# The attention output product of a one-core RWKV and feed-forward kernel in three fp32r passes, moved behind the first value tile

## The reference

```python
x = x + 0.5 * ffn(layernorm(x))            # ffn: one 256x256 matrix, summed from 8 chosen adapters, and a bias
x = x + attn(layernorm(x))
x = x + 0.5 * ffn(layernorm(x))

def attn(x):                               # x: 8 x 512 x 256
    h = layernorm(x) * ln1_g + ln1_b
    hh = time_shift(h)                     # the token before, zero for the first
    k, v = mix(h, hh, tm_k) @ Wk.T, mix(h, hh, tm_v) @ Wv.T
    sr = sigmoid(mix(h, hh, tm_r) @ Wr.T)
    rwkv = sr * wkv(time_decay, time_first, k, v)   # a scan over the tokens
    x = x + rwkv @ Wo.T                    # the output product of this case; its sum is xa below
    h = layernorm(x) * ln2_g + ln2_b
    hh = time_shift(h)
    kk = square(relu(mix(h, hh, cm_k) @ Wck.T))     # 1024 wide
    return x + sigmoid(mix(h, hh, cm_r) @ Wcr.T) * (kk @ Wcv.T)
```

## Time and profile before

| | |
|---|---|
| median of 3 runs | 430.83 us (430.48 to 431.03) |
| the profiled execution | 430.12 us, span of its instructions 428.0 us |
| TensorE clock granted over the span | 0.997 of full speed |
| PE busy | 414.6 us, 97% |
| DVE busy | 372.2 us, 87% |
| ACT busy | 334.7 us, 78% |
| POOL busy | 181.9 us, 43% |

### The profile page before, as it was taken

The page is one execution under the profiler, slowest core; times in us unless marked ns, Lnnn a source line. Parts: engine busy times, 40 slices in busy tenths (PEclk is TensorE's granted clock), DMA queues, the critical chain, the costliest instruction groups (busy, mean ns, idle before and its releaser), DMA issues.

```text
span 428.0 us, 6400 instructions
## 1 busy us (share of the span) xinstructions
PE 414.6 (97%) x2074; PEld 335.9 (78%) x2074; DVE 372.2 (87%) x735; ACT 334.7 (78%) x679; POOL 181.9 (43%) x194
## 2 busy tenths in 40 slices
PE   8989989989999999999999999999999999999996
PEld 8865875668867887798769886788779876988895
DVE  3988989997989899998989898989999898979555
ACT  1158977899699969998799969996999479956830
POOL 1446062817173454617281727345461518043011
PEclk9999999999999999999999999999999999999998
DMA  6991010001000001000200020000000000000011
GB/s 202 394 397 67 2 49 0 2 1 52 0 0 2 25 18 58 0 26 1 76 0 2 25 74 2 0 25 20 7 2 25 2 25 0 2 25 27 0 51 50
DMA packets 15971, 18.52 MB, mean 43 GB/s; under 512 B 1082, under 2 KB 13634, under 8 KB 15938
## 3 DMA queue, kind: packets, MB, share of 16 engines
q1 hardware_dynamic: 14538, 17.05, 11.3%
q10 hardware_dynamic: 1400, 1.07, 0.9%
HBM read 13.92 MB, written 4.19 MB: 42 GB/s over the span
## 4 chain that ended last, share of the span: by engine, by line
PE 75%; DVE 2%; issue 1%; POOL 1%; ACT 0%; DVEq 0%; POOLq 0%
PE pair L490 21%; PE pair L368 10%; PE pair L380 10%; PE pair L464 6%; PE pair L465 6%; PE pair L468 6%; PE pair L358 6%; PE pair L349 4%; PE pair L434 1%; PE pair L435 1%; PE pair L438 1%; PE pair L511 1%; PE pair L510 1%; PE pair L514 1%; PE pair L528 0%
## 5 line engine op out<-in xcount | busy, mean ns | idle before, releaser
L490 PE MATMUL pair<-wcv_sb,kk 128*128 128x256 f32 x448 | 100.4, 380 | 0.0
L490 PEld LDWEIGHTS pair<-wcv_sb,kk 128*128 128x128 f32 x448 | 83.8, 190 | 11.4 <-ACT kk L755 0.7
L464 PE MATMUL pair<-xck_hi,wck_hi 128*128 128x512 f32 x128 | 54.8, 428 | 0.0
L468 PE MATMUL pair<-xck_lo,wck_hi 128*128 128x512 f32 x128 | 50.7, 396 | 0.0
L465 PE MATMUL pair<-xck_hi,wck_lo 128*128 128x512 f32 x128 | 50.6, 395 | 0.0
L751 ACT ACTIVATE kk<-pair 128x512 f32<-128x512 f32 x64 | 36.3, 589 | 14.6 <-PE pair L468 14.5
L1407 POOL TENSOR_TENSOR x2b<-xs,bias_bc 128x512 f32<-128x512 f32 (+1 forms) x16 | 20.0, 1253 | 56.0 <-DVE xcr L1117 33.2
L755 ACT ACTIVATE kk<-kk 128x512 f32<-128x512 f32 x64 | 36.3, 624 | 0.0
L1407 POOL TENSOR_TENSOR x<-x,bias_bc 128x512 f32<-128x512 f32 x14 | 18.1, 1298 | 40.8 <-DVE xcr_lo L1165 22.3
L1447 POOL TENSOR_TENSOR xs<-x,xa 128x512 f32<-128x512 f32 x16 | 20.4, 1273 | 33.7 <-DVE xa L1098 33.7
L1433 POOL TENSOR_TENSOR xr<-xr,h 128x512 f32<-128x512 f32 x16 | 19.2, 1222 | 28.4 <-ACT xr L811 28.4
(11 more groups left out here) (181 smaller groups left out, 1135.1 us busy)
## 6 DMA issues: line engine op xcount, KB each, us to landing
x<-in_x_dram SPq DMA_DIRECT2D x8, 512.0 KB, 4.2
out_dram<-xs SPq DMA_DIRECT2D x15, 256.0 KB, 2.1
xt<-in_xt_dram SPq DMA_DIRECT2D x4, 512.0 KB, 7.4
work<-in_ffn_w_dram ACTq DMA_DIRECT2D x4, 256.0 KB, 4.3
work<-in_ffn_w_dram SPq DMA_DIRECT2D x4, 256.0 KB, 4.6
kk<-in_wck_dram SPq DMA_DIRECT2D x1, 1024.0 KB, 10.6
xs<-in_xt_dram SPq DMA_DIRECT2D x2, 512.0 KB, 11.6
wcv_sb<-in_wcv_dram SPq DMA_DIRECT2D x1, 1024.0 KB, 13.3
```

Source lines behind the costliest of these rows:

```text
L464: nc.tensor.matmul(key_bank(n), wck_hi[:, h, cols], xck_hi[:, h, :], start=h == 0, stop=False)
L468: last = nc.tensor.matmul(key_bank(n), wck_hi[:, h, cols], xck_lo[:, h, :], start=False, stop=h == CH - 1)
L490: last = nc.tensor.matmul(bank_of("kv", e, i)[:, t % TB * C:(t % TB + 1) * C], kk[:, n, tok:tok + P], wcv_sb[:, n, :], start=n == 0, stop= ...
```

## The change

Weights: `wo_sb` (already scaled by 0.5) gets a high part `wo_hi` (ACT, `setup_wo_high`, in the place of three constants of the start, which are gathered in the tile `early`) and a low part `wo_lo` (DVE, `output_weight_rest`, in place). Item 0 keeps the fp32 product. For items 1 to 7 `rwkv` gets a high part on ACT (`output_input_high`, two instructions between square 6 and square 7 of kk) and a low part on POOL (`output_input_rest`, two instructions, behind the second bias sum of x), and the product is 24 fp32r matmuls: for each of the two token tiles of a bank, the matmuls with `rwkv_hi` for both banks first, then those with `rwkv_lo`. Both banks are signalled by the last matmuls of the whole.

PE: `output_product(f)` stands behind the whole tile 0, `turn_xa(f)` in the middle of tile 2. ACT: squares 4 to 6 come before the high part of rwkv, square 7 and the residual before the gate's tanh; one of the squares of x2 moves behind the high part of xv. POOL: the bias sum into the second half of x2b (of item e - 1) moves from behind the small inverses to directly behind the inverse root of xa. Semaphores are merged where one could serve twice; such lines are left out below.

```diff
-        centre_own = sb("centre_own", [P, P])
-        centre_other = sb("centre_other", [P, P])
+        early = sb("early", [P, 2 * P + C])
+        centre_own, centre_other, bias_sel = early[:, 0:P], early[:, P:2 * P], early[0:K, 2 * P:2 * P + C]
...
+        wo_hi, wo_lo = in_place_of("early", "wo_hi", [P, CH, C]), in_place_of("wo_sb", "wo_lo", [P, CH, C])
...
+        rwkv_hi, rwkv_lo = in_place_of("xr", "rwkv_hi", [P, CH, T]), in_place_of("rwkv", "rwkv_lo", [P, CH, T])
...
             def output_product(f):
                 if f == 0:
                     pe.wait_ge(s_wo, 1)
-                pe.wait_ge(rwkv_done, 2 * f + 2)
-                to_tokens("o", rwkv, wo_sb, xa2_done, f, o_ps)
+                    pe.wait_ge(rwkv_done, 2 * f + 2)
+                    to_tokens("o", rwkv, wo_sb, xa2_done, f, o_ps)
+                    return
+                if f == 1:
+                    pe.wait_ge(s_wo_lo, 1)
+                pe.wait_ge(rwkv_hi_done, 2 * (f - 1) + 2)
+
+                for t in range(TB):
+                    toks = [slice((i * TB + t) * P, (i * TB + t + 1) * P) for i in range(BANKS)]
+                    dsts = [bank_of("o", f, i)[:, t * C:(t + 1) * C] for i in range(BANKS)]
+                    for i in range(BANKS):
+                        if t == 0:
+                            take(pair_of("o", f), i, xa2_done, 2 * f + i + 1)
+                        for h in range(CH):
+                            nc.tensor.matmul(dsts[i], rwkv_hi[:, h, toks[i]], wo_hi[:, h, :], start=h == 0, stop=False)
+                            nc.tensor.matmul(dsts[i], rwkv_hi[:, h, toks[i]], wo_lo[:, h, :], start=False, stop=False)
+                    for h in range(CH):
+                        if t == 0:
+                            pe.wait_ge(rwkv_lo_done, 2 * (f - 1) + h + 1)
+                        for i in range(BANKS):
+                            last = nc.tensor.matmul(dsts[i], rwkv_lo[:, h, toks[i]], wo_hi[:, h, :], start=False, stop=h == CH - 1)
+                            if t == TB - 1 and h == CH - 1:
+                                last.then_inc(o_ps, 1)
...
                 if e == LAST:
                     break
-
-                channel_values(e, 0, range(HB // 2))
+                channel_values(e, 0)
                 if has(f):
                     output_product(f)
-                channel_values(e, 0, range(HB // 2, HB))
                 channel_values(e, 1)
+
+                channel_values(e, 2, range(HB // 2))
                 if has(f):
                     turn_xa(f)
-                channel_values(e, 2)
+                channel_values(e, 2, range(HB // 2, HB))
...
+            def setup_wo_high():
+
+                act.wait_ge(s_ffn_ps, 1)
+                act.wait_ge(s_wo, 1)
+                nc.scalar.activation(wo_hi[:, :, :], wo_sb[:, :, :], ACT.Copy).then_inc(s_wo, 1)
+
+            def output_input_high(f):
+                act.wait_ge(r_ps, 2 * f + 2)
+                for h in range(CH):
+                    act.wait_ge(rwkv_done, 2 * f + h + 1)
+                    nc.scalar.activation(rwkv_hi[:, h, :], rwkv[:, h, :], ACT.Copy).then_inc(rwkv_hi_done, 1)
...
+                if h == 0 and 0 <= f - 2 < SUMS_X2:
+
+                    act.wait_ge(var_done["x2"], NT * (f - 2) + TB)
...
             keep_first(5)
+            setup_wo_high()
             setup_wv()
...
+                if has(f):
+                    value_input_high(f)
+                    scaled_difference(f)
                 if 0 <= e - 1 < SUMS_X2:
                     squares_x2(e - 1, (1,))
-                if has(f):
-                    value_input_high(f)
-                    scaled_difference(f)
...
                 for n in range(1, HB // 2):
                     key_square(e, n)
+                for n in range(HB // 2, HB - 1):
+                    key_square(e, n)
+                if has(f):
+                    output_input_high(f)
+                key_square(e, HB - 1)
+                if has(f):
+                    residual_of(f)
                 channel_gate(e)
-                if has(f):
-                    residual_of(f)
-                for n in range(HB // 2, HB):
-                    key_square(e, n)
...
+            def output_weight_rest():
+                dve.wait_ge(s_wo, 2)
+                dve.wait_ge(o_ps, CH)
+                nc.vector.tensor_tensor(wo_lo[:, :, :], wo_sb[:, :, :], wo_hi[:, :, :].bitcast(F32), ALU.subtract).then_inc(s_wo_lo, 1)
...
             norm_output(0)
+            output_weight_rest()
             stats_x1(1)
...
+            def output_input_rest(f):
+                for h in range(CH):
+                    pool.wait_ge(rwkv_hi_done, 2 * (f - 1) + h + 1)
+                    nc.gpsimd.tensor_tensor(rwkv_lo[:, h, :], rwkv[:, h, :], rwkv_hi[:, h, :].bitcast(F32), ALU.subtract).then_inc(rwkv_lo_done, 1)
...
                     bias_to_x(f + 1, 1)
+                if has(f):
+                    output_input_rest(f)
+                if has(f + 1):
                     lower("x1", f + 1 - SUMS_X1, x1_done, 2 * (f + 1) + 2)
                 if has(f):
                     attention_sum(f, 0)
                     attention_sum(f, 1)
                     inverse_std("xa", f)
+                if has(e - 1) and e < LAST:
+
+                    bias_to_x2(e - 1, 1)
                 if has(f + 1):
                     first_inverses(f + 1)
                 if has(f + 2):
                     inverse_x(f + 2)
-                if has(e - 1) and e < LAST:
-                    bias_to_x2(e - 1, 1)
```

28 lines of the change are left out of this document (14 added, 14 removed).

## The result

| | us, median (range), runs |
|---|---|
| before | 430.83 (430.29 to 431.06), 5 |
| changed | 443.38 (443.01 to 445.39), 5 |
| ratio | 1.030, 95% interval 1.0285 to 1.0314 |
| predicted | 439.1, range 433.3 to 442 |

The change makes the kernel 12.6 us slower, 4.3 more than predicted and outside the range. The profiled execution of the changed kernel took 445.39 (span 443.5); its other four have spans of 441.1 to 441.7, so about 2 us of it is this one execution's. They stand in the start: TensorE waited 2.33 us for its first `normed` (before 1.23), and behind that the granted clock from 24 to 32 us was 0.79 (before 1.00), so part of this stretch ran at 1.2 GHz instead of 2.4.

A forecast was written before the change was run, and what follows sets the result against it. TensorE, busy 97% of the span, was taken as the bound. Product -4.4, chain to the turned xa +11.4, tile 0 wait +1.2 and start +0.1 gave +8.3 us: 439.1 us predicted, range 433.3 to 442.

The forecast's parts named there:

- The chain from the product to the turned xa: Output product to xa's transposes: banks finishing together and the moved bias add holding up normalisation make TensorE wait, +11.4 us.
- The first rival: At xa's normalisation: GpSimd's bias add does not hold it up, giving 433.5 us; chance 9%.
- The product: Output product in items 1 to 7: 24 fp32r matmuls take 2.82 us instead of 3.45, -4.4 us.
- The 2.62 us: Output product time by the skill's 109 ns per matmul; not used, it would make the sum 1.4 us lower.
- The wait inside tile 0: Value tile 0: TensorE waits for ScalarE's eighth square, 0.2 us an item in items 2 to 7, +1.2 us.
- "No wait" for the low part: Output product: GpSimd's low parts of rwkv are ready in time, with 0.3 us to spare.
- The third rival: GpSimd's low parts meet VectorE's adds of the next x1, 0.5 us in seven items: 442.6 us; chance 9%.
- The start: Before item 0: VectorE's weight subtraction stands ahead of the mix, +0.1 us.
- The forecast's own range: Total time with the wait in tile 0 between its bounds: 437.5 to 441 us.
- Behind the turning there is room: After xa's transposes: mixing and high/low parts need about 4.7 us, TensorE has 5.18 of values first; nothing charged.

The follow-up runs named there:

- e15: Changed kernel with ScalarE's old order of the x2 squares and the output product done bank by bank: 434.76 us.
- e1: Changed kernel with GpSimd's second-half bias add for x2 put back behind the two small inverses: 446.12 us.
- e5: Kernel before, with only GpSimd's second-half bias add for x2 moved directly behind the inverse for xa: 433.08 us.
- e9: Changed kernel with one wait added: GpSimd's mixing of xr waits until both low parts of xv are done on VectorE: 439.89 us.
- e2: Changed kernel with the second half of the x2 squares back ahead of xv's high copy and the scaled difference on ScalarE: 439.34 us.
- e4: Kernel before, with only the x2 squares' second half moved behind xv's high copy and the scaled difference, plus the wait this needs: 430.62 us.
- e10: e3 with GpSimd's mixing of xr waiting for both low parts of xv: 440.38 us.
- e3: Changed kernel with both GpSimd's bias add for x2 and ScalarE's x2 squares back in their old places: 444.25 us.
- e16: e2 with xa turned after six of the third value tile's eight summands instead of four: 444.59 us.
- e17: e16 with the second token tiles of the output product done bank by bank: 441.26 us.
- e18: e17 with GpSimd's mixing of xr waiting for both low parts of xv: 436.19 us.
- e23: Changed kernel, old squares order, product bank by bank, rwkv's low part on VectorE, mixing of xr waiting for xv's low parts, xa turned after five summands: 430.53 us.

## Why the prediction was right and wrong

**The chain from the product to the turned xa (+11.4): right**, 11.5 measured, each link within 0.05 us in items 3 to 7. Item 2 lost 2.14 us instead of 1.83: its first add of xa starts 0.42 us behind the semaphore that it waits for, and not 0.07 as everywhere else. That is so in all twelve kernels in which GpSimd makes the low part of rwkv and in none of the others; no row says why. That alternating banks cost the other part is shown by e15, that the bias add costs the normalisation 0.94 us by e1 (turning 0.94 sooner) and by e5 (+2.3 us in the kernel before, as worked out from the same rows). The first rival's hope, that the order of the two might turn, did not come true in any item; but what it rests on, that the earlier start wins, decided elsewhere, below. By the Trainium skill, page SBUF - State Buffer, section Who interferes with whom, the instruction that issues first keeps the shared ports for its length; the traces agree in items 2 to 6 of all kernels and disagree in item 7 of three, with the numbers in the last section.

**The product (-4.4): right**, 2.82 us of matmuls; in the kernels without a wait the product takes 3.03, but tile 0 ahead of it is shorter by the same 0.2. The Trainium skill, page TensorE: Matmul & The Clock Gate, section Back-to-back issue gap, gives the 109 ns for an isolated matmul and says that in a stream of matmuls with weight loads both set the pace. The 2.62 us is an estimate from that figure; the trace has 117 ns and 2.82 us.

**The wait inside tile 0 (+1.2, bounds 0 to 3): the step that failed**, with its sentence "the mixing ahead of the scan comes some 0.2 us later in the new order, so I charge 0.2 us". It asks only when the mixing is ready, not what it starts beside. The mixing came earlier against VectorE, started 0.03 to 0.05 us ahead of the second xv_lo and held it up 1.1 us in items 3 to 6, and the scans were late by that. Tile 0 itself then lost 2.4 us, twice the term though within its bounds, and the product 0.7. The larger part is a term that the sum does not have at all: the late scans reach ScalarE's relu, and TensorE waits 2.7 us for it in the keys. These three make up the miss and put the time outside the range. e9 shows it by itself: with the meeting fenced and nothing else changed the kernel takes 439.9 us, 0.8 above the forecast, and e2 439.3. Without the meeting tile 0 and product lose 0.32 us an item in e2 and 0.44 in e9 rather than 0.2.

**"No wait" for the low part: nearly right**, 0.11 to 0.13 us an item. The third rival's meeting did occur in items 1 to 6 (VectorE's adds took 1387 and 1497 instead of 480 ns), though the forecast has the adds behind GpSimd's work. It cost little, since the adds are done before the product is (in item 5 at 295.55, E is 296.25).

**The start (+0.1)** can't be told: in the profiles of the changed kernels item 1's tile 0 begins anywhere from 91.5 to 94.3 us (in those of before, e4 and e5 from 91.6 to 92.4). The forecast's own range, said to be 437.5 to 441, should begin at 439.1 - 1.2 = 437.9; nothing hangs on it.

**"Behind the turning there is room": right for this kernel, and only with the bias add moved.** With it at its old place (e1, e10) the mixing of xk is held up instead, and where the kernel before had more than 1 us of room, the changed one has none: 24 matmul records of the values and not 32 now follow xa's turning. So the bias move cost 0.94 us an item and saved about as much; undoing it, which the forecast would have valued at 5.6 us, loses 2.7, and where the mixing is fenced it changes nothing clear of noise (e10 440.4, e9 439.9).

What stays open: that e3, e16 and e17 fall back into the meeting because VectorE's low parts of x2 keep xv_lo waiting is read from the traces, but no run changed that part by itself; and ScalarE's lateness in e18 and e23 (0.6 us in tile 0) was not traced to one instruction.
